# A three-layer interaction kernel: the prologue's weight copies, loads and splits rearranged

## The reference

```python
hidden = x
for i in range(3):
    z = jnp.einsum('bmd,bnd->bmnd', x, hidden).reshape(B, -1, D)   # 39*39 or 39*100 rows
    cur = jnp.einsum('bcd,co->bod', z, Ws[i]) + bs[i][None, :, None]   # 200 outputs
    cur = jax.nn.relu(cur)
    if i != 2:
        hidden, direct = (cur[:, :100, :], cur[:, 100:, :])
    else:
        direct = cur
    finals.append(direct)
return jnp.sum(jnp.concatenate(finals, axis=1), axis=-1)              # (512, 400)
```

## Time and profile before

| What | us |
|---|---|
| Median of 3 runs | 2790.56 (2789.16 to 2792.14) |
| The profiled execution, its own time | 2791.72 |
| Its span in the profile | 2790.0 |
| PE busy | 2702.3 (97%) |
| DVE busy | 2667.3 (96%) |
| ACT busy | 1698.4 (61%) |
| PE's first layer 1 matmul | at 84.11 |

### The profile page before, as it was taken

One profiled execution on the slowest core, in us unless ns is written; L12 is line 12 of the kernel. 1 busy time (PEld: TensorE's weight loads), 2 busy tenths in 40 slices (PEclk: granted clock), 3 DMA queues, 4 the chain that ended last, 5 costly groups with the idle time before them and its releaser, 6 DMA issues.

```text
span 2790.0 us, 56206 instructions
## 1 busy us (share of the span) xinstructions
PE 2702.3 (97%) x18112; PEld 2661.2 (95%) x18112; DVE 2667.3 (96%) x3218; ACT 1698.4 (61%) x3179; POOL 1.2 (0%) x11
## 2 busy tenths in 40 slices
PE   1799999999999999999999999999999999999999
PEld 1799999999999999999999999999999999999998
DVE  3799999999999999999999999999999999999997
ACT  2566666666666666666666666666666666666664
POOL 0000000000000000000000000000000000000000
PEclk9999999999999999999999999999999999999999
DMA  8454544454554454454454454445444445444541
GB/s 194 109 128 110 129 122 108 120 133 108 125 128 109 114 139 109 115 131 115 108 136 117 109 128 124 108 125 128 108 121 122 118 116 132 112 111 123 127 108 59
DMA packets 346786, 333.97 MB, mean 120 GB/s; under 512 B 151970, under 2 KB 281614, under 8 KB 346638
## 3 DMA queue, kind: packets, MB, share of 16 engines
q1 hardware_dynamic: 346762, 333.67, 48.0%
HBM read 332.73 MB, written 8.37 MB: 122 GB/s over the span
## 4 chain that ended last, share of the span: by engine, by line
PE 82%; DVE 8%; issue 4%; DMA 3%; ACT 2%; SPq 1%; DVEq 0%; ACTq 0%
PE acc L659 51%; PE acc L660 24%; PE acc L647 5%; DVE z_low L384 4%; DVE z L380 2%; DMA xb<-x_by_unit 1%; PE summed L677 1%; PE turned L671 1%; ACT z_high L525 1%; DMA xb<-in_L_rec_b_dram 1%; DVE z L361 1%; ACT hid L544 0%; DMA w_rows_again<-in_L_rec_W_dram 0%; DMA xb<-in_L_rec_W_dram 0%; DVE w_split L349 0%
## 5 line engine op out<-in xcount | busy, mean ns | idle before, releaser
L659 PE MATMUL acc<-w_split,z_high 128*128 128x400 f32 (+1 forms) x8320 | 2511.8, 369 | 64.6 <-DVE z_low L384 58.5
L660 PE MATMUL acc<-w_split,z_low 128*128 128x200 f32 (+1 forms) x8320 | 2120.5, 255 | 0.0
L525 ACT ACTIVATE z_high<-z 128x1024 fp32r<-128x1024 f32 (+3 forms) x1152 | 1125.0, 977 | 882.4 <-DVE z L380 728.3
L659 PEld LDWEIGHTS acc<-w_split,z_high 128*128 128x128 f32 (+1 forms) x8320 | 1565.4, 188 | 88.5 <-issue 78.4
L660 PEld LDWEIGHTS acc<-w_split,z_low 128*128 128x128 f32 (+1 forms) x8320 | 1593.0, 191 | 0.0
L384 DVE TENSOR_TENSOR z_low<-z,z_high 128x1024 fp32r<-128x1024 f32 (+3 forms) x1152 | 1282.5, 1113 | 45.3 <-ACT z_high L525 45.0
L380 DVE TENSOR_TENSOR z<-hid,xb 128x1024 f32<-128x1024 f32 (+2 forms) x1024 | 1142.0, 1115 | 11.2 <-DMA xb<-x_by_unit 10.9
L544 ACT ACTIVATE hid<-turned 32x128 f32<-32x128 f32 x768 | 205.3, 267 | 8.9
L541 ACT ACTIVATE hid<-turned 96x512 f32<-96x512 f32 x256 | 150.4, 588 | 91.8 <-PE turned L671 91.6
L647 PE MATMUL acc<-w_whole,z_whole 128*128 128x200 f32 x1024 | 197.7, 336 | 3.1 <-DVE s L391 3.1
L647 PEld LDWEIGHTS acc<-w_whole,z_whole 128*128 128x128 f32 x1024 | 168.9, 190 | 3.4 <-DVE s L391 3.4
(11 more groups left out here) (25 smaller groups left out, 72.0 us busy)
## 6 DMA issues: line engine op xcount, KB each, us to landing
xb<-x_by_unit SPq DMA_DIRECT2D x384, 384.0 KB, 4.4
x_right<-x_by_unit SPq DMA_DIRECT2D x384, 136.5 KB
xb<-x_by_unit SPq DMA_DIRECT2D x384, 128.0 KB, 5.0
xb<-x_by_unit SPq DMA_DIRECT2D x128, 336.0 KB
xb<-x_by_unit SPq DMA_DIRECT2D x128, 84.0 KB
x_left<-x_by_unit SPq DMA_DIRECT2D x384, 19.5 KB
xb<-in_L_rec_W_dram SPq DMA_DIRECT2D x6, 600.0 KB, 9.4
x_by_unit<-in_r_x_dram SPq DMA_DIRECT2D x128, 19.5 KB
```

The costliest lines, as they stand in the source:

```text
L525: nc.scalar.activation(z_high[slot][0:rows, 0:n * T], z[slot][0:rows, 0:n * T], ACT.Copy).then_inc(high, 1)
L659: nc.tensor.matmul(a[:, 0:2 * O], z_high[slot][0:rows, tok], w, start=(c == 0), stop=False, skip_group_check=True)
L660: last = nc.tensor.matmul(a[:, 0:O], z_low[slot][0:rows, tok], w[:, 0:O], start=False, stop=(c == chunks - 1), skip_group_check=True)
```

## The change

- The copies of W0 hold only rows of fields 13 to 38 (26 rows) with 20 repeated. Pairs of fields 0 to 12 are read from the input itself, ahead of the wait for the copies. So there are twelve loads for pair_w and pair_w2, six of 13 rows and six of 26 rows.
- pair_w and pair_w2 lie in the z ring, which is now one tensor. x of unit 0 can so come to xb[0] at once, and does so group by group behind the pieces of W1.
- W1's pieces 0 and 1 are staged in a new area, stage2, and pieces 2 and 3 in xb[1]; none waits for a split. W2's pieces all go through stage2. The output rows lie in stage2 as well.
- PE waits for W1 alone ahead of layer 1 of unit 0. W2's pieces are rounded and subtracted inside periods 0 (piece 0) and 1 (pieces 1 to 3), with the `stage_zeros` of W2. PE waits for them ahead of the first layer 2.
- Some operations that stood between periods 0 and 1 (`sums`, `directs`, `second_half`, the low part of layer 0 of unit 2, `transpose`) now stand inside period 1, behind its first products or groups.

```diff
-    w0c = nc.dram_tensor("w0_columns_again", [F, 2 * F, O], F32)
-    w0r = nc.dram_tensor("w0_rows_again", [2 * F, F, O], F32)
+    w0c = nc.dram_tensor("w0_columns_again", [REST, REST + WRAP, O], F32)   # REST 26, WRAP 20, NEAR 13
+    w0r = nc.dram_tensor("w0_rows_again", [REST + WRAP, REST, O], F32)
@@ SP
+            def load_w0(near):
+                f0, n = (0, NEAR) if near else (NEAR, REST)
+                cols, rows = (w0, w0) if near else (w0c_t, w0r_t)
...
+            for to, at, n in ((0, NEAR, REST), (REST, 0, WRAP)):
+                sp.dma_start(bass.AP(w0c_t, to * O, [[(REST + WRAP) * O, REST], [1, n * O]]), ...
+                sp.dma_start(bass.AP(w0r_t, to * REST * O, [[REST * O, n], [1, REST * O]]), ...
+            sp.wait_ge(cleared, 2)
+            load_w0(True)
+            sp.dma_start(pair_w[L0_ONES:L0_ROWS, 0, :], ...
             sp.wait_ge(xt_done, 32)
             sp.wait_ge(ones_l0, 2)
             load_pairs(0)
-            turn_x(0, 1)
             sp.wait_ge(w0_again[0], 32)
             sp.wait_ge(w0_again[1], 32)
+            load_w0(False)
+            turn_x(0, 1)
+            sp.wait_ge(ones_set, 1)
+            for g in range(2):
+                load_w(sp, 1, g, W1, b1)
+                load_xb(0, 0, g)
             sp.wait_ge(xt_done, 64)
             turn_x(0, 2)
             sp.wait_ge(product, 1)
             load_pairs(1)
+            for g in range(2, GROUPS):
+                load_w(sp, 1, g, W1, b1)
+                load_xb(0, 0, g)
             sp.wait_ge(xt_done, 96)
             turn_x(0, 3)
+            for g in range(2):
+                sp.wait_ge(w_low_done, g + 2)
+                load_w(sp, 2, g, W2, b2)
+            sp.wait_ge(product, 2)
+            load_pairs(2)
             sp.wait_ge(xt_done, 128)
             turn_x(1, 0)
+            sp.wait_ge(w_low_done, 5)
             sp.wait_ge(ones_set, 2)
             for g in range(GROUPS):
                 sp.wait_ge(xb_in[g], XB_COUNT[g])
                 load_xb(1, 1, g)
+            for g in range(2, GROUPS):
+                sp.wait_ge(w_low_done, g + 4)
+                load_w(sp, 2, g, W2, b2)
@@ DVE, behind layer 0 of unit 2 in period 0
+            low_piece(5, 2, 0)
@@ DVE, period; second is true in period 1 alone
                 product12(1, n, par, 0, base, slot(0))
+                if second:
+                    lows(base - 1, slot(-1), L0_ROWS, L0_CHUNKS)
+                    sums(1, 0)
...
                 product12(1, n, par, 1, base + 1, slot(1))
                 lows(base, slot(0), P, group_chunks(0))
+                if second:
+                    sums(0, 2)
+                    directs(1, 0, 0)
+                    low_piece(6, 2, 1)
+                    dve.wait_ge(w_low_done, 7)
+                    stage_zeros(2)
                 product12(1, n, par, 2, base + 2, slot(2))
                 lows(base + 1, slot(1), P, group_chunks(1))
+                if second:
+                    directs(0, 0, 2)
+                    low_piece(7, 2, 2)
                 product12(1, n, par, 3, base + 3, slot(3))
                 lows(base + 2, slot(2), P, group_chunks(2))
...
+                if second:
+                    low_piece(8, 2, 3)
                 product12(2, n - 1, 1 - par, 0, base + q, slot(q))
@@ ACT, period
                 highs(base, slot(0), P, group_chunks(0))
+                if second:
+                    second_half(1, 0, base - 2)
                 highs(base + 1, slot(1), P, group_chunks(1))
+                if second:
+                    second_half(0, 2, base - 1)
+                    dup(1, 0)
+                    high_piece(2, 1)
+                    dup(0, 2)
                 highs(base + 2, slot(2), P, group_chunks(2))
+                if second:
+                    hidden(1, 0, 0)
+                    high_piece(2, 2)
...
                     highs(base + 4, slot(4), L0_ROWS, L0_CHUNKS)
+                if second:
+                    high_piece(2, 3)
@@ PE
-            pe.wait_ge(w_low_done, 1 + 2 * GROUPS)
-            pe.wait_ge(w_whole_in, 1)
+            pe.wait_ge(w_low_done, 1 + GROUPS)
...
                 multiply(1, base + 1, slot(1), 1)
+                if second:
+                    transpose(1, 0)
+                    transpose(0, 2)
...
+                else:
+                    pe.wait_ge(w_low_done, 1 + 2 * GROUPS)
+                    pe.wait_ge(w_whole_in, 1)
                 multiply_whole(n - 1, 1 - j % 2)
```

More of the change, by code:

```diff
@@ L115, in cin_kernel @@
         direct = {l: sb(f"direct{l}", [P, DIRECT[l]]) for l in range(3)}
-        o_row = {l: sb(f"o_row{l}", [BT, DIRECT[l]]) for l in range(3)}
+        stage2 = sb("stage2", [P, 2 * GROUP * O])
+        o_row = {l: stage2[0:BT, OUT_AT[l]:OUT_AT[l] + DIRECT[l]] for l in range(3)}
         acc = {l: bank(f"acc{l}") for l in range(3)}
@@ L206, in load_xb @@
                       .then_inc(xb_in[g], 16)
[L208 to L223, removed]
@@ L418, in _ @@
+            dve.wait_ge(w_low_done, 1)
             product0(0, 0, 0)
             lows(0, 0, L0_ROWS, L0_CHUNKS)
[L420 to L435, removed]
@@ L436, in _ @@
-            dve.wait_ge(w_low_done, 1 + 2 * GROUPS)
-            nc.vector.memset(xb[1][MAIN:P, TAIL_AT:CHUNKS, :], 1.0).then_inc(ones_set, 1)
+            low_piece(1, 1, 0)
+            sums(0, 0)
+            low_piece(2, 1, 1)
+            product0(1, 1, 1)
+            lows(1, 1, L0_ROWS, L0_CHUNKS)
+            directs(0, 0, 0)
+            low_piece(3, 1, 2)
+            sums(0, 1)
+            low_piece(4, 1, 3)
+            dve.wait_ge(w_low_done, 5)
+            ones(1)
             directs(0, 0, 1)
@@ L447, in _, with period @@
             lows(at + 3, slot_of(at + 3), P, group_chunks(3))
[L448 to L454, removed]
+            low_piece(5, 2, 0)
+            def period(m, j, base, sl, layer0=True, before0=True, before2=True):
                 n, par = m * QUARTERS + j, j % 2
@@ L495, in period @@
                     sums(0, n + 2)
-            period(0, 1, first(1), first(1) % RING, before2=False, last_low=False)
+            period(0, 1, first(1), first(1) % RING, before2=False)
             period(0, 2, first(2), first(2) % RING)
@@ L524, in highs @@
                 act.wait_ge(product, number + 1)
-                nc.scalar.activation(z_high[slot][0:rows, 0:n * T], z[slot][0:rows, 0:n * T], ACT.Copy).then_inc(high, 1)
+                nc.scalar.activation(z_high[slot][0:rows, 0:n * T], z[0:rows, slot, 0:n * T], ACT.Copy).then_inc(high, 1)
             def second_half(l, u, last):
@@ L557, in _ @@
             highs(0, 0, L0_ROWS, L0_CHUNKS)
[L558 to L575 removed]
+            high_piece(1, 0)
+            second_half(0, 0, 0)
+            act.wait_ge(consts, 4)
+            dup(0, 0)
+            high_piece(1, 1)
+            hidden(0, 0, 0)
+            highs(1, 1, L0_ROWS, L0_CHUNKS)
+            high_piece(1, 2)
+            second_half(0, 1, 1)
+            dup(0, 1)
+            high_piece(1, 3)
             at = first(0)
@@ L702, in period @@
                 acc_free(1, n)
+                second = not before2
                 multiply(1, base, slot(0), 0)
-                if before0:
+                if before0 and not second:
                     transpose(0, n + 1)
```

163 lines of the change are left out of this document (82 added, 81 removed).

## The result

The changed kernel takes 2776.89 us (median of 5 runs, 2774.93 to 2777.11) against 2789.94 (5 runs, 2789.16 to 2792.14) beside it: ratio 0.995, 95% interval 0.9935 to 0.9965, 13.05 us less. The forecast was 12.3 less. The profiled execution took 2776.07, its span is 2774.3.

What follows compares the result with a forecast made beforehand. PE was taken to bound the body, which stays; 27.3 us won ahead of PE's first layer 1 matmul minus 14.95 lost behind it gave 12.3 less: 2779.4 us profiled, 2778.3 against the median, range 2768 to 2786.

Steps and rivals of the forecast that it cites:

- The body stays: From period 2 on, the 125 or so periods, bound by PE, stay at 21.08 us each.
- Copies 12.0, pair loads 21.7, W1 48.7, T1 56.8: Prologue landing times in us; T1, PE's first layer 1 matmul, comes at 56.8, which is 27.3 earlier.
- The rule of engines by row count: W1's tail loads: DMA engines are the largest divisor of outer dimensions up to 16; 1 to 2 us, left out.
- T2 - T1 = 55.5: From PE's first layer 1 matmul (T1) to its start of period 2 (T2): 55.5 us, 14.95 more than before.
- The cold second group: PE's second group of period 1, after 5.3 us idle, runs mostly at 1.2 GHz: 3.98 us instead of 2.35.
- xb[1] and W2 hidden: Behind T1, transfers of xb[1] and W2's pieces land before they are wanted; thinnest cover 2 us.
- Rival A: Period 1 stalls are shorter, PE at full clock: T2 - T1 46 to 50, 20 us gained, 2770.8; chance 0.18.
- B: Prologue loads come later, at 179 GB/s: T1 60 to 62, gain 6 us, 2784.5; chance 0.14.
- C: PE stays at 1.2 GHz through the rest of period 1: T2 - T1 65, gain 2 us, 2788.5; chance 0.06.
- D: DVE loses its lead and bounds the body: slower, 2802 us at 0.6 us of waits a period; chance 0.05.
- The sum: Whole kernel: 27.3 earlier at T1 minus 14.95 behind it, 12.3 us less, 2779.4 for the profiled execution.

Runs made afterwards that it cites:

- e5: Changed kernel with W0 copied whole again (3.68 MB instead of 1.91): 2784.37 us, one run.
- e11: The changed kernel unaltered, profiled and timed again: 2776.10 us (4 runs), ratio 0.9947 to the kernel before.
- e1: Changed kernel with PE's two transposes of period 1 ahead of its second group: 2772.98 us, one run.
- e3: Changed kernel rounding and subtracting only one chunk of each W2 piece, output not the reference's: 2768.64 us, one run.
- e2: Changed kernel with ACT rounding W2's third piece ahead of hidden(1,0): 2776.78 us, one run.
- e4: Changed kernel with 22 and 30 matmuls without a reader in PE's two idle stretches of period 1: 2774.20 us, one run.
- e8: Changed kernel with period 1 reordered, most W2 pieces behind the products and lows PE waits for: 2762.70 us (4 runs), ratio 0.9903 to the kernel before.
- e7: Changed kernel with all of W2 loaded, rounded and subtracted ahead of layer 1 of unit 0, through stage2: 2774.97 us, one run.
- e12: The kernel of e7 timed four times: 2776.82 us, ratio 0.9949 to the kernel before.
- e10: As e9, with GpSimd also subtracting W2's pieces 1 to 3: 2766.91 us (4 runs), ratio 0.9913 to the kernel before.
- e9: As e8, with GpSimd instead of DVE clearing the staging area for W2's last piece: 2763.87 us (4 runs), ratio 0.9902 to the kernel before.

## Why the prediction was right, point by point

- **The body stays.** Right: PE busy for 2620.16 of 2621.00 us.
- **Copies 12.0, pair loads 21.7, W1 48.7, T1 56.8.** Measured 12.58, 23.48, 48.83, 56.91. The pair loads were 1.8 late, past the 21 to 23 named as a sign, and the rest faster by as much: 25.35 us for 5.16 MB and two turns where I had 27.0. The errors cancelled, they were not small each. With 21.7 from the bytes and 222 GB/s T1 would have come out at 55.4. That T1 fell within 0.1 is luck: it scatters from 55.6 to 57.7. e5 shows that bytes ahead of the pair loads reach T1 in full; its 6.7 us for 1.77 MB is dearer than the 5.2 of the sum, of which its copies took 4.2. (The 0.43 MB of pairs queued behind the copies are 13*39*800 bytes = 0.41; nothing in the sum hangs on it.)
- **The rule of engines by row count** (the Trainium skill, DMA: Bandwidth & Descriptors, "Why a DMA increments its semaphore by 16 and not by 1") would have put W1's last piece 1 to 2 us behind 48.7; it came at 48.83. Nothing here needs the rule, but with errors of 1.7 us in the terms around it this does not speak against it either.
- **T2 - T1 = 55.5.** Measured 54.2, 55.8 on the second execution. Step by step behind T1, predicted and measured: layer 0 on PE 13.0, 12.3; second low's group 23.8, 22.95; third piece subtracted 31.4, 30.95; third group 35.5, 34.97; z_whole 40.85, 40.36; T2 55.5, 54.2 (the sum's own terms give 55.6). The first 0.7 is that the rounding of layer 0, which waits for PE, was at 6.5 and not 7.2: PE's pairs behind T1 were 0.55 us apart for 5.0 us in the profile before, from which the offset was taken, and for 3.3 in this one. Of the 0.7, 0.5 are left at z_whole, and 0.8 more come behind it. In e11, with 6.1 us at the low clock, PE began 1.3 earlier and T2 was 0.3 later, so a microsecond either way is the execution's. e1 to e3 moved T2 where the chain says, if in e1 and e2 by somewhat less than expected, so the chain was the cause and not a coincidence of sums.
- **The cold second group**, 3.98 expected, 4.39 measured; taken away in e4 it gave 1.4 at T2 and 1.9 from the group's start on, where the term was worth 4.0 - 2.35 = 1.65 in the sum. The idle stretch ahead of it was 4.95 us, where 5 or more was named as a sign.
- **xb[1] and W2 hidden.** Right: between T1 and T2 no wait of DVE or ACT was ended by a DMA.
- **Rival A** asked for T2 - T1 of 46 to 50; the order didn't give it, e8 did and went past it. **B**: the landing was on time. **C**, the whole of period 1 cold: the third group was at 1.2 GHz until about 97.6, but layer 0 and layer 2 from 99.70 ran at 1.00, so no. The rule by which each burst restarts cold (the Trainium skill, TensorE: Matmul & The Clock Gate, "HAM oscillation — how this bites in real kernels") is told there of bursts with waits of several microseconds between them. The gaps of 4.95 and 7.24 us agree with it; those of 0.48 to 1.42 us were not followed by the low clock, and the forecast's rival C had stretched the rule to them. **D**: DVE kept up, the body has the old length.
- **The sum.** T2 moved by 13.6 where the sum had 12.3, nearly all of the difference in T2 - T1. The medians moved by 13.05, and the profiled execution took 2776.07 where 2779.4 was forecast: 1.3 of these 3.3 are T2, the other 2 the body's scatter. That the medians came within 0.8 of the forecast is better than its terms are.

What the forecast didn't ask is which part of the change makes the gain. It put the late W2 split inside one sum with the loads and so didn't see that it is worth nothing as ordered. It had the price behind T1, 14.95 us, but never summed what the same loads and splits of W2 would take ahead of T1 through stage2; that is 15.8 us (e7).

## What to carry to other kernels

Work that is moved from a prologue into a full pipeline is not priced by its length alone but by its place in each queue. Here 7.5 us of the loss went with the split work and the rest were waits. With the same work in an order that puts the pipeline's own products first, the stretch took 40.7 us instead of 54.2, some 3 us more than without the work (37.8 and 38.3 in e12 and e7). Ask for each part of a change what it earns where it leaves and what it costs where it arrives; the late split of W2 earned 15.8 and cost 15.9. Follow such a piece through all engines with offsets from one point; here that came within 1.3 us and showed which position to change. An idle engine that works in the shadow of a full one has to be looked at together with it: GpSimd's subtractions stopped DVE for as long as they took.

## What was not expected of the hardware

- How long PE stays at 1.2 GHz behind an idle stretch is not set by the length of that stretch alone in these profiles. Behind 4.60 us (e8), 4.57 (e10) and 2.90 (e9) the granted clock was 0.50 until about 87.8, 92.2 and 90.2, for 4.1, 6.5 and 6.4 us of work. Behind 7.80 and 7.42 us the changed kernel took 3.3 us in one profile and 6.1 in the other. So a gain of a microsecond or two ahead of such a gap can be lost by the execution. Why the clock came back later in some no run tells.
- GpSimd's subtraction of 128x1600 took 4.0 to 4.5 us where DVE takes 1.82, and its memset of 32x1400 1.26, as DVE's 1.23.
